# Attention: keys and queries are restacked through a DRAM copy, with 10 DMAs a unit in place of 24

## What is computed

```python
Q = split_heads(layernorm(x) @ Wq.T + bq)        # 16 heads of 32
K = split_heads(ctx @ Wk.T + bk)
V = split_heads(ctx @ Wv.T + bv)
scores = einsum('bhqd,bhkd->bhqk', Q, K) / sqrt(32)
x = x + einsum('bhqk,bhkd->bhqd', softmax(scores), V) @ Wo.T + bo
x = x + top-2-of-8-experts(layernorm(x))
```

## Time and profile before

| | |
|---|---|
| Median of 3 runs | 1720.36 us (1716.99 to 1723.82) |
| The profiled execution | 1732.28 us |
| Its span, first to last instruction | 1730.5 us, mean granted clock 0.970 |
| PE busy | 1597.8 us (92%) |
| DVE, POOL, ACT busy | 1272.5, 837.5, 658.1 us |
| Attention | about 0 to 985 us; experts after that |

### The profile page before, as it was taken

One profiled execution on the slowest core, in us unless ns is written; L12 is line 12 of the kernel. 1 busy time (PEld: TensorE's weight loads), 2 busy tenths in 40 slices (PEclk: granted clock), 3 DMA queues, 4 the chain that ended last, 5 costly groups with the idle time before them and its releaser, 6 DMA issues. The chain is left out here.

```text
span 1730.5 us, 30244 instructions
## 1 busy us (share of the span) xinstructions
PE 1597.8 (92%) x9612; PEld 1168.4 (68%) x9612; DVE 1272.5 (74%) x2414; ACT 658.1 (38%) x1267; POOL 837.5 (48%) x634
## 2 busy tenths in 40 slices
PE   6889999999899999999998469999999999999995
PEld 4445555555555555555553259999999998999994
DVE  5575777878668778687685668778888778777873
ACT  3354544535445445354444133223323234222320
POOL 3364656566566676566678321423333333423232
PEclk9999999999999999999999769999999999999997
DMA  6342333443434433424331161324543253324321
GB/s 221 84 121 66 106 112 85 112 104 88 121 80 111 103 94 94 116 75 110 92 99 33 56 223 50 101 85 166 172 147 123 87 204 121 107 85 149 116 86 61
DMA packets 101125, 188.99 MB, mean 109 GB/s; under 512 B 28192, under 2 KB 29600, under 8 KB 100960
## 3 DMA queue, kind: packets, MB, share of 16 engines
q1 hardware_dynamic: 79936, 124.25, 25.4%
q0 software_dynamic: 20832, 62.49, 11.4%
q10 hardware_dynamic: 192, 0.26, 0.0%
HBM read 204.32 MB, written 37.51 MB: 140 GB/s over the span
## 5 line engine op out<-in xcount | busy, mean ns | idle before, releaser
L802 DVE TENSOR_REDUCE negmax<-max_ps 128x2 f32<-128x1024 f32 x252 | 307.4, 1220 | 175.5 <-PE max_ps L542 174.1
L671 ACT ACTIVATE pt<-work 128x512 f32<-128x512 f32 x512 | 278.6, 595 | 263.5 <-PE work L554 256.7
L983 POOL TENSOR_TENSOR acc<-acc,pt 128x1024 f32<-128x1024 f32 x128 | 303.8, 2377 | 134.1 <-ACT pt L671 134.1
L1486 PE MATMUL gu_ps<-xgT_hi,wg_hi 128*128 128x256 f32 x1248 | 349.3, 280 | 2.3 <-DVE xgT_lo L1601 1.5
L1486 PE MATMUL gu_ps<-xgT_lo,wg_hi 128*128 128x256 f32 x1248 | 345.8, 277 | 0.0
L1486 PE MATMUL gu_ps<-xgT_hi,wg_lo 128*128 128x256 f32 x1248 | 345.5, 277 | 0.0
L980 POOL TENSOR_TENSOR acc<-pt 128x1024 f32<-128x1024 f32 x64 | 153.3, 2396 | 200.2 <-PE work L574 132.0
L1486 PEld LDWEIGHTS gu_ps<-xgT_hi,wg_hi 128*128 128x128 f32 x1248 | 235.2, 188 | 3.0 <-issue 1.9
L1747 POOL DMA_INDIRECT out<-acc,token_of x78 | 77.2, 989 | 330.4 <-DVE acc L1645 324.6
L1486 PEld LDWEIGHTS gu_ps<-xgT_lo,wg_hi 128*128 128x128 f32 x1248 | 235.5, 189 | 0.1
L1486 PEld LDWEIGHTS gu_ps<-xgT_hi,wg_lo 128*128 128x128 f32 x1248 | 235.2, 188 | 0.0
(11 more groups left out here) (221 smaller groups left out, 2902.2 us busy)
## 6 DMA issues: line engine op xcount, KB each, us to landing
raw_g<-w_gate_up SPq DMA_DIRECT2D x39, 2048.0 KB
raw_d<-w_down SPq DMA_DIRECT2D x39, 1024.0 KB
qs<-q_hi SPq DMA_DIRECT2D x252, 64.0 KB
ks<-k_hi SPq DMA_DIRECT2D x252, 64.0 KB
bd<-b_down SPq DMA_DIRECT2D x39, 256.0 KB
x_in<-x SPq DMA_DIRECT2D x36, 256.0 KB, 3.3
ctxT_raw<-ctx_t SPq DMA_DIRECT2D x32, 256.0 KB, 4.1
xln_dram<-x SPq DMA_DIRECT2D x32, 256.0 KB, 2.8
```

What stands on the lines that cost most here:

```text
L671: e.activation(pt[k % 2][:, h, :], in_work("exp", u, k, h)[:, :], ACT.Exp, scale=scale).then_inc(exped.sem, 1)
L802: e.tensor_reduce(negmax[:, u % 2, n:n + 2], pair_of(u, r)[:, :, :], AX.X, ALU.max, negate=True).then_inc(maxed.sem, 1)
L983: e.tensor_tensor(acc[:, heads, :], acc[:, heads, :], pt[k % 2][:, heads, :], ALU.add).then_inc(added.sem, 1)
L1486: ins = e.matmul(gu_ps[n % GU_BANKS][:, part, :], wg[s][pw][:, k, cols], xgT[s][px][:, k, :], start=(k == 0 and m == 0), stop=(k == KD - 1 ...
```

## The change

Keys and queries of unit 1 and later no longer go from SBUF to SBUF head by head. Each part (k high, k low, q high, q low) is written whole to a DRAM tensor of 128 x 512 f32 in one DMA of 256 KB (`lay_down`). When that has landed, SP issues one DMA for each place where the part is wanted, which reads the DRAM tensor with the 4 heads side by side and writes 32 partitions x 4 x 512, also 256 KB (`pick_up`): two for a high part, one for a low part. Per unit that is 4 laid down and 6 picked up. Each stacking step on SP now has a wait in its middle, for the landing of its own lay-down, and a wait at its start, for the previous unit's pick-ups from the same DRAM tensor. ACT and DVE wait for the lay-down of the unit before, where they waited for its stacking. Unit 0 is as it was, with its semaphores renamed.

```diff
-            stacked[n] = Mark(sem(f"{n}_stacked"), [(0, 0), *[(u, i) for u in units[1:] for i in range(2)]], 16 * GROUP)
-            stacked_lo[n] = Mark(sem(f"{n}_stacked_lo"), units[1:], 16 * GROUP)
-            first_hi[n], first_lo[n] = sem(f"{n}_first_hi"), sem(f"{n}_first_lo")
+            hi_laid[n], lo_laid[n] = Mark(sem(f"{n}_hi_laid"), units[1:], 16), Mark(sem(f"{n}_lo_laid"), units[1:], 16)
+            stacked[n] = Mark(sem(f"{n}_stacked"), units[1:], 16 * 2)
+            stacked_lo[n] = Mark(sem(f"{n}_stacked_lo"), units[1:], 16)
+            first_top[n], first_hi[n], first_lo[n] = (sem(f"{n}_first_{part}") for part in ("top", "hi", "lo"))
...
+        parts_dram = {(n, part): nc.dram_tensor(f"{n}_{part}_dram", (P, S), F32, kind="Internal").ap() for n in "kq" for part in ("hi", "lo")}
+
+        def lay_down(e, n, part, source, landed):
+            e.dma_start(parts_dram[n, part], source[:, :].bitcast(F32)).then_inc(landed, 16)
+
+        def pick_up(e, n, u, row, part, landed):
+            e.dma_start((qs if n == "q" else ks)[u % RING][HD * row:HD * (row + 1), :, :].bitcast(F32),
+                        parts_dram[n, part].rearrange("(h p) s -> p h s", h=GROUP)).then_inc(landed, 16)
...
             def qk_hi(n, u):
                 e.wait_ge(projected[n].sem, projected[n][u])
-                if u:
-                    e.wait_ge(stacked[n].sem, stacked[n][u - 1, 1 if u > 1 else 0])
-                if u == 1:
+                if u > 1:
+                    e.wait_ge(hi_laid[n].sem, hi_laid[n][u - 1])
+                elif u:
+                    e.wait_ge(first_top[n], FIRST)
                     e.wait_ge(first_hi[n], FIRST)
...
             def qk_lo(u, n):
                 e.wait_ge(hi_made[n].sem, hi_made[n][u])
                 if u > 1:
-                    e.wait_ge(stacked_lo[n].sem, stacked_lo[n][u - 1])
+                    e.wait_ge(lo_laid[n].sem, lo_laid[n][u - 1])
...
             def stack_hi(n, u):
                 e.wait_ge(hi_made[n].sem, hi_made[n][u])
+                if u == 0:
+                    stack(e, n, 0, HIGH_AT[n][0], hi[n], first_top[n])
+                    return
+                if u > 1:
+                    e.wait_ge(stacked[n].sem, stacked[n][u - 1])
+                lay_down(e, n, "hi", hi[n], hi_laid[n].sem)
                 if u >= RING:
                     e.wait_ge(exp_ready.sem, exp_ready[u - RING, T - 1, GROUP - 1])
-                for part in HIGH_AT[n][:2 if u else 1]:
-                    stack(e, n, u, part, hi[n], stacked[n].sem)
+                e.wait_ge(hi_laid[n].sem, hi_laid[n][u])
+                for row in HIGH_AT[n]:
+                    pick_up(e, n, u, row, "hi", stacked[n].sem)
 
             def stack_lo(n, u):
                 e.wait_ge(lo_made[n].sem, lo_made[n][u])
+                if u > 1:
+                    e.wait_ge(stacked_lo[n].sem, stacked_lo[n][u - 1])
+                lay_down(e, n, "lo", lo[n], lo_laid[n].sem)
                 if u >= RING:
                     e.wait_ge(exp_ready.sem, exp_ready[u - RING, T - 1, GROUP - 1])
-                stack(e, n, u, LOW_AT[n], lo[n], stacked_lo[n].sem)
+                e.wait_ge(lo_laid[n].sem, lo_laid[n][u])
+                pick_up(e, n, u, LOW_AT[n], "lo", stacked_lo[n].sem)
```

## The result

| | before | after |
|---|---|---|
| Median | 1722.09 us (1716.99 to 1723.84, 4 runs) | 1844.29 us (1832.56 to 1851.01, 4 runs) |
| Ratio | | 1.0708, 95% interval 1.0647 to 1.0768 |
| The profiled execution | 1732.28 us | 1832.56 us |
| Start of the last `turn_max` | 926.8 us | 1031.9 us |
| PE's idle time at the first row maximum of a unit, 31 steps added up | 17.5 us | 95.0 us |

The change makes the kernel 122 us slower; 1717 us with a range of 1704 to 1740 was forecast. The last two lines of the table are read from the trace, one `turn_max` and the row maximum behind it per step. The two profiled executions show 100.3 of these 122 us, since before's is slower than all four runs of its median, and after's is the fastest of its four. In them the whole loss is there by the last `turn_max`: it comes 105.1 us later (the first one comes 1.8 us later already).

What follows compares the result with a forecast made beforehand. PE's own order was taken as the bound, DMAs costing only where PE waits; -8.6 - 5.0 + 2.5 + 2.0 = -9.1 on the profiled 1732.3 gave 1723.2, the median 1711.3 to 1723.6, middle 1717, range 1704 to 1740 us.

Steps and rivals of the forecast that it cites:

- the room: Time from the high part made to the end of turn_max: 11.4 us in queries-first steps, 12.3 in keys-first steps.
- step 1: DMA issues on SP: 24 a unit become 10, the chain's 12 become 5 at 0.6 us each, -4.2 us.
- step 5: Picking up the low part from DRAM: taken as 3.5 us to landing, ends 2.8 and 4.7.
- the chain as a whole: From high part made to last landing, with SP's lateness: 11.4 us queries first, 10.8 us keys first.
- the slower rival: Round trip longer than the room, at the first row maximum of queries-first and early units: 1732 us; chance 0.25.
- Step 2: Laying down the high part in DRAM: taken as 2.0 us, ends 2.0 and 2.8, with the queue empty.
- (4): Laying down the low part, issued behind the first pick-ups: taken as 3.5 us, ends 2.0 and 4.5.
- The sum's gain of 8.6 + 5.0 us: PE's three waits under "issue" fall away, -8.6 us, and the clock lost in the two longest, -5.0.
- Slow issues: SP's issues still slow at times: 10/24 of today's in six queries-first units, +0.4 us each, +2.5.
- nothing at all: Rival: SP only idles, chain length and slow issues stay; 1720 to 1722 us, counted with the main case of 0.50.
- Parts at no cost: SP's new waits, ACT's and DVE's waits and added DMA time cost nothing; DMA share rises to about 0.47.
- The 2.5 us put on a long wait: Clock lost by PE after unit 16's wait of 4.2 us, whose step was 6.7 us longer.

Runs made afterwards that it cites:

- run 1: The changed kernel with 46 of the scatters to token_list moved behind the last unit; start of the last turn_max 952.6 us, against 1031.9.
- run 2: The changed kernel with the scatters to token_list in round 1 of a step in place of round 3; 1849.09 us, ratio 1.0742.

## Why the prediction was wrong

**What held.** The bound (PE, and PE's wait at the first row maximum), the room (11.4 us, measured again in run 1), the direction of the issues (step 1: 1.8 us for five, where 3.0 was priced), the pick-up of the low part (step 5: 3.5 taken, 2.8 to 3.3 measured in nearly all) and, in the keys-first steps, the chain as a whole when nothing holds it (10.8 taken, 11.1 to 13.2 measured without scatters, against a room of 12.3 or more). The DMA share was no bound. The sites of the slower rival were right, the first units and the queries-first ones, and its mark in the profile (over 1 us at every fourth unit) is there.

**Step 2 failed, the lay-down of the high part, 2.0 us with an upper end of 2.8, "the queue is empty then".** It is 2.0 only for the first one of a step without scatters. What counts is the second pair's, and its queue isn't empty: 3.0 to 3.8 us in keys-first steps from unit 8 on, and 3.5 to 5.0 in the five queries-first steps where it stands behind a load of x and a store of `xln`. There it is 4.3 on average, 2.3 more than taken, the largest single miss of the sum. Two more terms miss in these steps: SP comes 0.7 to 2.6 us late, 1.7 on average, where 0.5 was taken, and the low lay-down (4) takes 3.8 to 5.6, 4.7 on average, where 3.5 was taken. With (5) at -0.5 and the issues at -0.4 the chain is 15.1 us, not 11.4, and the room was 11.4 as read. In the example of unit 20 it is 14.0, with 5.0 for the lay-down.

The slower rival has its 40 us from a chain 2.6 us longer, and the changed kernel without scatters costs 38.7. That the two agree is partly luck: the rival had 14 us of waits in 13 keys-first units, where 1.8 came, and 26 in ten others, where 31.4 came, 22.8 more than in before without scatters; and it had no clock, while PE is busy 16.4 us longer with the same instructions. Its mechanism and its sites were right; it was priced at its middle, 15, with a chance of 0.25. The sum's gain of 8.6 + 5.0 us couldn't come while the chain was longer than the room.

**The larger half, 66 us, was in no case.** Behind the scatters the first lay-down of a step takes 4.3 to 8.1 us. The thought that kept it out is the one under the slower rival, "single DMAs in this trace land close to their medians". That was read from medians over the whole run, which can't show it; the trace of before had loads of x that landed in 7.1 to 8.1 us, in a stretch of 4 us, with nobody waiting. The stores and loads whose tail I did look at the earlier trace rows were taken one by one and read as an effect of what stood before them on SP's queue, not on POOL's.

**"Slow issues" were taken for a matter of the number of issues.** The earlier trace rows shows 9.77 us for 8; the scatters stand at 447.59 and 449.17 us on POOL, beside them, and I didn't look there. The prediction let this cost shrink with the number of issues (10/24). It is tied to the scatters, which already held landings back in before, where nobody waited; with the change nothing over 1.9 us is left among SP's issues, but the landings are waited for. The rival "nothing at all" had half of it: the slow issues have to do with time and not with number, but they didn't stay.

**"Parts at no cost".** "That cover holds as long as no transfer is waited for that isn't now" was the right condition, and the change breaks it by construction: four landings per unit become things SP waits for, in one line for both pairs, so that a late `k_hi` moves `q_lo`. In unit 14 4.7 us of late landing were followed by 5.3 us of PE idle, ten DMAs later.

**Clock.** A step that waits 7.19 us is 9.8 us longer than without (36.8 against 27.0), one that waits 5.33 is 6.4 longer (37.0 against 30.6). The 2.5 us put on a long wait in the prediction were right for the first and too much for the second. In all, PE is busy 33.4 us longer with the same instructions, at a granted clock of 0.93 in place of 0.98, so about a third of the loss is clock. The prediction's sum had clock only as a gain, of 5.0 us.

**Two rules of the Trainium skill.** The one on coalescing ("DMA: Bandwidth & Descriptors", "Rules for kernel authors") was followed here, and the kernel became slower by the ratio 1.07: fewer and larger DMAs, at the price of a landing in the chain. The one on ports ("SBUF — State Buffer", "Door 1: The DMA port swizzle") can't be judged: pick-ups of low parts to 32 partitions nearly all land in 2.8 to 3.3 us without scatters, which leaves open whether their data took 1.1 or 1.4.

**Left open.** Why the scatters are confirmed so late, what sets it between 7 and 13 us from the first one's start, and why the data behind them slows down, no run separates. The change costs 122 us by medians and 100 in the profiled pair; where the other 22 lie can't be read from these two traces. Nor was a scatter of other sizes tried, or the list written in another way than by scatter.

## What to carry to other kernels

Before you put a landing into an in-order chain, read the worst landings of that stretch and not the median of the run, on every queue: a small scattered write from another engine can hold up landings behind it for many times its own length. Trading issues for a round trip can pay only where the issues are longer than the landing that replaces them; no case here paid (the high parts, 8 issues or 4.9 us, came close with a ratio of 1.007; the low parts, 4 issues or 2.4 us, cost 62.5 us). A hold-up that a schedule hides may not be free to move; each place tried here had its own victim, `k_hi`, `k_lo`, `q_lo` and the row maxima in turn.

## What the runs showed of the hardware

- Two scatters of 128 x 4 bytes to DRAM, 1 us each on POOL, keep the landings of DMAs issued behind them on SP's queue outstanding until 6 to 14 us after the first one's start (median 8.5 in the changed kernel, 10.0 in run 2); with one it is 6 to 9 (median 7.2), with four 19 in the step shown. In run 2 each such landing comes 0.2 to 2.3 us after the last increment of the scatters' own semaphore.
- With a single DMA behind them its data has long moved (share 0.00 in the 1.8 us before the landing). With many, the data is held as well: in the kernel before 45 GB/s for 3 us, with 98 ahead of that and 251 behind it, and 1 GB/s for 4 us in unit 16's step.
- It concerns transfers from SBUF to SBUF as well (6.2 to 9.2 us where 2.0 is usual), and at times SP's issuing: one issue of 5.40 us with the scatters, and none over 2.1 without.
- A store of 256 KB to DRAM takes 2.0 us to landing on an empty queue, and 3.5 to 5.0 behind one load and one store (five steps of the changed kernel without scatters).
- ACT needs 0.62 us for one DMA issue, as SP does, and with 248 of them moved to ACT the last `turn_max` of a PE-bound attention comes 133 us later (1059.9 against 926.8).
